# Lower message halves ahead of the second layer's work on VectorE, in a two-layer graph and expert kernel

## What is computed

```python
x = x + gnn0(ln(x))   # segment_sum(edge_weight * (ln(x) @ wl)[src], dst) + ln(x) @ wr + biases
x = x + ffn0(ln(x))   # sum over 8 experts: gate_e * (relu(bn(relu(bn(y @ W1_e)) @ W2_e)) @ Wo_e + bo_e)
x = x + gnn1(ln(x))   # segment_sum(edge_weight * (ln(x) @ weight)[src], dst) + bias
x = x + ffn1(ln(x))   # 32 experts, argmax picks one per node
```

## Time and profile before

| | |
|---|---|
| median of three runs | 3012.72 us |
| profiled execution, its own time | 3008.19 us |
| its span in the trace | 3006.3 us |
| TensorE matmul busy | 2719.2 us (90%) |
| VectorE busy | 2165.6 us (72%) |
| ScalarE busy | 1514.5 us (50%) |
| GpSimd busy | 1939.8 us (65%) |

### The profile page before, as it was taken

One profiled execution on the slowest core, in us unless ns is written; L12 is line 12 of the kernel. 1 busy time (PEld: TensorE's weight loads), 2 busy tenths in 40 slices (PEclk: granted clock), 3 DMA queues, 4 the chain that ended last, 5 costly groups with the idle time before them and its releaser, 6 DMA issues. The chain is left out here.

```text
span 3006.3 us, 53462 instructions
## 1 busy us (share of the span) xinstructions
PE 2719.2 (90%) x18949; PEld 2484.4 (83%) x18949; DVE 2165.6 (72%) x5008; ACT 1514.5 (50%) x3146; POOL 1939.8 (65%) x1692
## 2 busy tenths in 40 slices
PE   5799935899999999999999993689999999999999
PEld 5789825788888888888888873689999999999998
DVE  8898836577777877877787655767777777777762
ACT  4377636788888888888888651111111111111111
POOL 0355557777777777777777204777777777777750
PEclk9999956899999999999999996789999999999999
DMA  2133454333333233333323105888888888788860
GB/s 73 6 80 77 91 141 143 92 97 94 96 108 110 79 111 111 97 94 109 107 81 108 46 22 159 210 209 201 215 215 207 208 206 211 195 204 208 203 153 15
DMA packets 241570, 390.22 MB, mean 130 GB/s; under 512 B 43258, under 2 KB 114834, under 8 KB 241042
## 3 DMA queue, kind: packets, MB, share of 16 engines
q0 software_dynamic: 163072, 310.24, 40.6%
q1 hardware_dynamic: 77940, 74.90, 7.9%
q10 hardware_dynamic: 288, 1.61, 0.1%
HBM read 343.43 MB, written 43.19 MB: 129 GB/s over the span
## 5 line engine op out<-in xcount | busy, mean ns | idle before, releaser
L1324 POOL DMA_INDIRECT f_got<-h_tab,list_cols x784 | 974.9, 1244 | 287.8 <-issue 220.2
L1994 POOL DMA_INDIRECT n_got<-h_tab,edge_cols x784 | 798.9, 1019 | 263.2 <-issue 232.3
L2046 ACT ACTIVATE n_hrh<-bank 128x512 fp32r<-128x512 f32 (+1 forms) x208 | 119.3, 574 | 924.5 <-PE bank L2116 924.5
L1609 DVE TENSOR_TENSOR f_hlo<-edge_cols,f_hhi 128x1024 fp32r<-128x1024 f32 (+1 forms) x208 | 241.8, 1162 | 300.0 <-ACT f_hhi L1414 299.4
L2095 PE MATMUL bank<-n_got,n_hot_h 128*128 128x256 f32 x1168 | 352.0, 301 | 70.1 <-DMA n_got<-h_tab,edge_cols 36.2
L1384 ACT ACTIVATE f_got<-f_got,list_cols 128x256 f32<-128x256 f32 x784 | 333.9, 497 | 150.2 <-DMA f_got<-h_tab,list_cols 150.1
L1495 PE MATMUL bank<-f_mhi,f_hot 128*128 128x256 f32 x1168 | 316.2, 304 | 80.8 <-DVE f_mlo L1603 80.8
L1409 ACT ACTIVATE edge_cols<-bank,f_shf,f_scl 128x512 f32<-128x512 f32 (+1 forms) x416 | 295.2, 744 | 118.5 <-PE bank L1315 84.8
L2096 PE MATMUL bank<-n_got,n_hot_h 128*128 128x256 f32 x1168 | 338.6, 290 | 0.0
L2097 PE MATMUL bank<-n_got,n_hot_l 128*128 128x256 f32 x1168 | 338.5, 290 | 0.0
L2197 DVE TENSOR_SCALAR n_hot_h<-list_cols,rel_f,edge_cols 128x256 fp32r<-128x256 f32 (+1 forms) x784 | 252.4, 389 | 117.2 <-PE bank L2097 117.1
(11 more groups left out here) (327 smaller groups left out, 7396.3 us busy)
## 6 DMA issues: line engine op xcount, KB each, us to landing
f_got<-h_tab,list_cols POOLq DMA_INDIRECT x784
n_got<-h_tab,edge_cols POOLq DMA_INDIRECT x784, 3.8
h_tab<-acc SPq DMA_DIRECT2D x37, 128.0 KB
edge_cols<-in_w SPq DMA_DIRECT2D x16, 256.0 KB, 3.2
xn<-acc_tab SPq DMA_DIRECT2D x8, 512.0 KB, 5.8
n_rows<-acc_tab SPq DMA_DIRECT2D x8, 512.0 KB, 5.6
out_rows<-n_rows SPq DMA_DIRECT2D x8, 512.0 KB, 4.6
acc<-in_x SPq DMA_DIRECT2D x4, 896.0 KB, 8.4
```

Source lines behind the costliest of these rows:

```text
L1324: nc.gpsimd.indirect_dma_start(got[:, s % RING0, u, :], None, h_tab[0], bass.IndirectOffsetOnAxis(gidx0[:, s * U + u:s * U + u + 1], 0), b ...
L1609: nc.vector.tensor_tensor(hlo[l][:, :, 0:w], rl[:, :, 0:w], hhi[l][:, :, 0:w].bitcast(F32), ALU.subtract).then_inc(s_lo[l], 1)
L1994: nc.gpsimd.indirect_dma_start(got[:, s % RING, u, :], None, h_tab[1], bass.IndirectOffsetOnAxis(gidx[:, s * U + u:s * U + u + 1], 0), bou ...
```

## The change

In the even slots in which VectorE makes the second layer's lower half (`s in AT[2]`, slots 12 to 194, 92 of them), it makes the lower messages of the next slot first of all. Before, they came behind `add_out`, the one-hot matrix and that lower half. All other slots and engines keep their order, and no instruction is added or removed.

```diff
                 for s in range(SLOTS):
+                    first = s in AT[2] and s + 1 < EGROUPS
+                    if first:
+                        lower_messages(s + 1)
                     if s in AT[4]:
                         add_out(AT[4][s], s)
                     if s - 1 in USE_AT and USES[USE_AT[s - 1]][1] == "bias":
                         output_bias(USE_AT[s - 1], s)
...
                     if s in AT[2]:
                         lower_half(1, AT[2][s])
                     if s - 1 in USE_AT and USES[USE_AT[s - 1]][1] == "prod":
                         lower_product(USE_AT[s - 1])
-                    if s + 1 < EGROUPS:
+                    if s + 1 < EGROUPS and not first:
                         lower_messages(s + 1)
                     if s in AT[0]:
                         lower_half(0, AT[0][s])
```

## The result

The changed kernel takes 3050.13 us (median of four runs, 3045.81 to 3050.83) where the kernel before takes 3012.06 beside it: a ratio of 1.0121, 95% interval 1.0101 to 1.0142, 38 us slower. A second comparison gave 3053.97, ratio 1.0136 (1.0092 to 1.0180). The prediction was 3030, its range ended at 3045. The direction was right, the size too small.

The account below looks back on a forecast made before the run. TensorE was taken to bound the kernel, with VectorE's loop through `rl` taking over after the edit. Loop 9.3, head-of-queue wait 9.2, second wait 0 and outside pairs 3.1 gave 21.6 us over 3008.2, so 3030; range 3008 to 3045.

Parts of the forecast that it names:

- The loop through `rl`: Second stage: VectorE and ScalarE wait on each other over one buffer; 9.3 us over the stretch; 12 to 37 slower, chance 0.58.
- The signs of the loop: Nine groups: L1495 waits below 8 us, L1313 waits over 25, ScalarE waiting in nearly all 72 pairs, groups about 106.6.
- the shortest turn: From one L1609's end through ScalarE's ReLU to the next L1609's start: 2.61 us, charged for each of 72 pairs.
- the sum: Slowdown added up as 9.3 + 9.2 + 0 + 3.1 = 21.6 us; its loop part is VectorE's work, turns and other waits.
- The head-of-queue wait: Slots like 146: moved L1603 waits 1.02 us for late upper messages, once in each of nine groups, 9.2 us.
- the port: VectorE's two-input instructions block GpSimd's gathers: 1.01 us alone, 1.96 beside L1603; gathers taken as long as now.
- A second wait of that kind: Slot 148: ReLU starts 1.35 us after L1609 because of a late gather; taken as 0, bound 9 x 1.35 = 12.2.
- xlo and gates: VectorE's waits at L1711 and L1661, 14.8 and 6.9 us in the stretch, kept as they were.
- 1 us shorter per slot: Gathers shorten, so the 9.2 us wait vanishes and the result is 12 us slower; within a rival of chance 0.28.

Follow-up runs that it names:

- four buffers: Ring `got` of gathered rows has four buffers instead of three, third layer's lower weights not kept: changed kernel 3005.79 us (0.9978), kernel before 2983.91 (0.9913).
- two `rl`: Changed kernel with a separate `rl` buffer for each layer, third layer's lower weights not kept: 3001.58 us, ratio 0.9971 to the kernel before.
- the last order: Changed kernel with L1626 and L1677 moved behind the second layer's L1609, three gather buffers: 3015.88 us, ratio 1.0011 to the kernel before.
- the late burst: Changed kernel with SyncE's burst of stores and one load per group starting one slot later: 3046.87 us, ratio 1.0113 to the kernel before.

## Why the prediction was off

**The loop through `rl`: right.** The signs of the loop came: TensorE's waits for messages fell below 8 (4.9), those before L1313 rose over 25 (33.1), idle time ahead of the second layer's L1609 all but vanished (33.6 to 2.3 us), the shortest turn is 2.61 us. Two did not: a group took 981.91 / 9 = 109.1 us, not 106.6, and the profile puts ScalarE's wait down to L1609 in 46 places, not in nearly all of 72 (with four buffers it is 69). With the ring out of the way the edit costs 21.0 us of stretch, against 9.3 + 9.2 = 18.5 in the sum. That closeness is partly luck: the sum's stretch was 959.9 and the measured one 939.3, and the kernel before got shorter by the fourth buffer as well.

**The head-of-queue wait: right in size by luck.** The profile has 6.3 us in 12 waits where I had 9 x 1.02 = 9.2. But in slots like 146, for which I had worked it out, L1603 waits in one group of nine (0.78). The others are nine waits of 0.32 in slots like 140 and two of 1.20 and 1.43 in slots like 148. The gather of slots like 147 had become shorter (see the port, below).

**The step that failed: "A second wait of that kind".** I took nothing for slots like 148, because VectorE's lateness there would be larger than the wait. Term by term, the stretch predicted and measured: work 741.0 and 736.0; turns 188 and 187.9; xlo and gates 21.7 and 10.8 + 4.6 = 15.4; L1603 9.2 and 6.3; waits for L1609 beyond the turn 0 and 224.2 - 187.9 = 36.3. Only the last is off by much. Of it, 9 x (5.87 - 2.61) = 29.3 are slots like 148 and 9 x 0.42 = 3.8 slots like 146. My bound of 12.2 was too low as well, because it took one slot for nine.

Most of this wait was not new. Added up over the 72 pairs of the kernel before, the turns from one L1609 to the next are 224.8 us, 36.9 more than 72 times 2.61, and 9 x (4.86 - 2.61) = 20.2 of these are slots like 148. There VectorE's free time paid for them. The sum priced every turn at the shortest one, so it dropped them just when the free time went; after the edit the turns add up to 221.9. In slots like 148 the edit added 9 x 1.01 = 9.1 us; in all other slots together the excess shrank from 16.7 to 4.7. The fourth buffer is the test: with it all 72 turns are 2.61, and the whole 36.3 us are gone.

The reasoning behind the zero was wrong in a way that slot 148 shows. VectorE's lateness couldn't cover the late gather here, because the gather starts from VectorE. The gather of slot 147 in the changed kernel and the L1603 ahead of it:

```profile
1382.09 1.16 POOL L1324 DMA_INDIRECT f_got<-h_tab,list_cols  x1 [4.13 <-DVE f_mlo L1603]
...
1407.61 1.01 POOL L1324 DMA_INDIRECT f_got<-h_tab,list_cols  x1 [0.30 <-DVE f_mlo L1603]
```

```profile
1380.02 2.35 DVE L1603 TENSOR_TENSOR f_mlo<-f_got,f_mhi 128x1024 fp32r<-128x1024 f32 x2
```

The first of this pair is the L1603 of slot 144; it ends about 1381.24, and the gather starts 0.85 us later, as in the kernel before (1353.42 to 1354.28). From there VectorE needs 1410.86 - 1381.24 = 29.6 us to the end of the L1609 in slot 148; before it was 1383.23 - 1353.42 = 29.8. So VectorE isn't late against the gather: its lateness has moved the gather along with it. The gathers' way got longer instead. GpSimd runs four slots of gathers back to back, from 1382.09 to 1408.62, and ScalarE can begin with slot 150's at 1413.12: 31.0 us. Before, this was 1382.96 - 1354.28 = 28.7 us, by ScalarE's row ahead of the earlier trace rows:

```profile
1382.96 1.72 ACT L1384 ACTIVATE f_got<-f_got,list_cols 128x256 f32<-128x256 f32 x4 [0.99 <-DMA f_got<-h_tab,list_cols]
```

Of the 2.3 us more, 1.3 are the gathers' instructions (their last one ended at 1379.54 before) and 1.1 the landing. Here too slot 148 is at the far end: in the mean of nine groups the gathers' way grew from 29.6 to 30.8 us, and VectorE's went from 29.8 to 30.0. Why the instructions and the landings got longer is not shown.

**Gathers that start in lumps: seen, but not shown as a cause.** In the kernel before, an L1603 stood at the end of every slot. In the changed one the odd slot's stands at the start of the even slot, directly behind the even slot's. The distance from one L1603's end to the next, mean by kind of slot, was 4.4 to 9.2 us and is 1.1 to 4.8 and 8.9 to 13.9 in turn. With three buffers each release starts one gather. So the waits at the gathers of slots like 147 rose from 2.35 to 3.86, like 155 from 1.59 to 2.67, like 145 from 0 to 1.90 (each without the 0.3 us that stand ahead of every gather): 4.5 us per group, as much as the group grew. It is tempting to call this the cause. Two runs with the ring of three and the same kind of lumps speak against it: with two `rl` the distances are 1.1 to 5.2 and 8.7 to 12.5, GpSimd waits only 29.1 us and the stretch is 941.2; in the last order they are 1.1 to 5.9 and 7.5 to 12.8, the waits are 119.5, and it is 947.8. What these two have and the changed kernel doesn't is slack in the loop. What the runs show is that the full loss takes both, a loop without slack and a ring of three whose gathers land late in one slot of each group; take either away and it is gone or halved. How much of the lateness comes from the lumps stays open. I had the row of the 2.81 us wait in hand and used it for one slot.

**The clock: not foreseen, small.** TensorE now stops for 3.9 us ahead of the second layer of slots like 133. TensorE's timeline, and the windows around it:

```profile
1308.82 0.80 PE L1313 MATMUL bank<-f_hhi,f_whi 128*128 128x512 f32 x1 [3.92 <-DVE f_hlo L1609]
...
1310.27 0.63 PE L1313 MATMUL bank<-f_hhi,f_whi 128*128 128x512 f32 x1
1310.70 0.63 PE L1314 MATMUL bank<-f_hlo,f_whi 128*128 128x512 f32 x1
```

```profile
1304.90:1308.80 3.90, 0.00 (x1) 0.00 (x0) 1.32 (x2) 3.87 (x7) 3.02 (x3) 0.76 0.37 107
1308.80:1312.20 3.40, 3.38 (x8) 2.70 (x9) 3.30 (x7) 2.60 (x5) 2.26 (x2) 0.50 0.27 77
1312.20:1315.60 3.40, 3.40 (x13) 2.64 (x12) 3.34 (x6) 1.84 (x3) 2.49 (x4) 0.77 0.28 80
```

Behind the stop the granted clock is 0.50, the lower level of 1.2 GHz, and the matmuls stand 0.43 us apart. The Trainium skill (TensorE: Matmul & The Clock Gate, Part 1) gives 426.7 ns as the distance of such matmuls on the cold array; the trace agrees. The stretch has a mean clock of 0.98 against 1.00. That it costs little is suggested by the run with the late burst: clock 1.00 throughout, stretch 977.0, still 35.6 over the kernel before. What share of the remaining 5 is the clock's stays open.

**The port: level in the mean, but not in slots like 147.** Gather instructions take 721.85 / 578 = 1.249 us after and 721.61 / 576 = 1.253 before, so the rival's "1 us shorter per slot" didn't come. In slots like 147 it did: from the start of the first of the four instructions to the end of the last it was 7.44 us and is 5.90 now (means of nine). In the kernel before, one of them stood beside the L1609 and L1603 that followed each other directly (1355.52 to 1357.87), and lasted 3.16 us; the changed kernel has no such pair there.

```profile
1355.59 3.16 POOL L1324 DMA_INDIRECT f_got<-h_tab,list_cols  x1 [0.30 <-issue]
```

That is the slot on which the head-of-queue wait hung, and the wait went with it, as this rival had said: the upper messages of slot 147 are ready at 1392.52 and its L1603 starts at 1393.03 with no wait. Over the runs the mean instruction goes from 667.35 / 578 = 1.155 us to the 1.324 of the last section, so the time of the gathers does depend on the order. Set beside VectorE's timeline, the cause is plain: in the stretch before the edit all 146 gather instructions that met none of VectorE's L1597, L1603, L1609 and L1711 took 1.01 or 1.02 us, and all 175 that took over 1.3 us overlapped one of these.

**Still open.** On the other chip the two orders with four buffers stood the other way round (0.9992 and 1.0038, intervals that just touch). Their profiled stretches of nine groups are nearly equal there (971.6 and 973.4 us), so the 21 us of the first chip are missing, and most of the difference between the two lies outside the stretch. Why is not known; that chip was not profiled with the plain changed kernel.

## What to carry to other kernels

When a loop through another engine takes over, price it by its turns as they stand, added up over the whole stretch, and not by its shortest turn. Here the difference was 36.9 us, hidden while VectorE had free time. Ask of each long turn what it waits for: a wait for a transfer stays when the free time goes. One slot doesn't stand for its kind; 148 had 1.35 us where the nine had 2.31. When an instruction is moved, list everyone who waits for it, not only who waits behind it; L1603 feeds TensorE and also frees the buffer for a gather three slots on. And where one engine's lateness is to cover another's wait, check that the other doesn't start from the first.

## What the runs showed of the hardware

A gather with a burst of SyncE's transfers beside it took 4.4 us from its last instruction to ScalarE's use, and 1.93 with the burst moved away (slots like 150, means of nine, ScalarE waiting in both). The Trainium skill (DMA: Bandwidth & Descriptors, "SWDGE vs HWDGE vs iDMA") says that each DMA engine goes round its queues in turn, and that transfers issued by GpSimd (SWDGE) and by SyncE (HWDGE) feed different ones of them; a gather that shares its engines with a burst would then land late, and the trace agrees.

With four buffers and no waits the gathers' instructions themselves got longer, 763.69 / 577 = 1.324 us in place of 1.253, so that GpSimd's queue stays full: 763.7 + 159.8 + 16.2 = 939.7 of 939.3 us. The rule is the one of the port above: the 155 that met none of VectorE's instructions with two inputs took 1.01 to 1.03 us, and all 227 over 1.3 us overlapped one. Why more of them meet in this order was not looked into.
